# Four groups of row copies ahead of one store, and one load for eight counts

## The chip, the core and the metric

The kernel runs on one core of a Trainium2 chip. The metric is the device time of one execution in microseconds. The core has five engines with instruction streams of their own: TensorE (PE; its weight loads are shown as PEld), VectorE (DVE), ScalarE (ACT), GpSimd (POOL) and SyncE (SP). They wait for each other through semaphores. SP computes nothing: it issues DMA transfers, loads registers and waits. GpSimd issues the gathers whose addresses come from a list of indices.

## The reference

Two graph layers, each added to its input and layer-normed:

```
# layer 0: x (12500,256), 200000 edges src -> dst sorted by dst, 4 heads of 16
ZU = einsum('nd,kdr->knr', Z, U);  zs = ZU[:, src];  zd = ZU[:, dst]
logits = (zs * zd).sum(-1) / sqrt(16)
alpha  = segment_softmax(logits, dst)                  # over the edges of one dst
agg    = segment_sum(alpha[..., None] * zs, dst)
Z_half = 0.5 * Z + 0.5 * einsum('k,knr,kdr->nd', softmax(head_w), agg, U)
DZ = Z_half @ Dmat.T;  residual = Z_half - DZ @ Dmat
x = layernorm(x + relu(Z_half + 0.5 * (residual @ Dmat) - 0.05))
# layer 1: weights from the first 6250 edges' heads, rows xt[dst] of x @ weight
x = layernorm(x + broadcast(einsum('nh,nhd->nd', softmax4(...)[:n], xt[dst[:n]])))
```

What the change touches is the edge part of layer 0: each of the 200000 edges needs the 64 numbers of its source node (256 bytes).

## The kernel before, in words

The edges are cut into tiles of 128 (1563 of them), the nodes into 98 tiles of 128. A *step* pairs one edge tile with one node tile; an edge tile whose edges end in two node tiles has two steps, so there are 1661 steps. The program goes over them in `NB = 52` *blocks* of `B = 32` steps, and a block in `NG = 4` *groups* of `G = 8` steps. Blocks are handled in turn in two halves `h` of every buffer; each engine's code for a block is a function (`period` on TensorE, VectorE and ScalarE, `turn` on SP), and blocks 2 to 47 run in a loop on SP of two blocks a trip (`turn(2 * i + h, ...)`, L483 on), the last four without a loop.

The way of a source row, and who waits for whom:

- GpSimd (L564 to L577) gathers the source rows of an edge tile from the table in DRAM into `ring`, which holds 32 tiles. It gathers in groups `q` of 8. From the fifth on it waits until enough groups of steps have been copied out (`copied`, against a count from the row `frees`).
- SP copies each step's tile from its slot in `ring` to the block's own buffer `zs` (`copy_steps(b, h, g, uses)`, L420 to L444): it waits until TensorE has summed the block before last that far (`sums_ps`), loads the eight slot numbers into registers with one load (L425), loads two counts of gathers (L431, from the row `needs`) and waits for them on the two semaphores `tiles_in` (L434), and issues eight copies (L437). Then it waits for the copies of the group before and raises `copied` for it (`landed`, L415 to L418).
- VectorE (`period`, from L945) makes the head products of the four groups (L902: `zs` times the destination rows in PSUM), then a chain of short steps that goes back and forth with TensorE: running maxima of the logits, at whose end L1012 raises `x_ready`. ScalarE takes the exponentials (L1607), VectorE scans the sums of the block before (L931), weighs `zs` (L1026) and splits it in three bf16 parts (L1031, L1036).
- TensorE expands the destination rows for the head products of the next block (`expand`, L1347, 24 matmuls a group) and adds the weighted rows up by node (`add_up`, L1364), in the order expand 0, expand 1, add_up 0 to 4, expand 2, add_up 4 to 6, expand 3, add_up 6 to 8.
- Beside this runs the dense part of layer 0: each block multiplies two tiles of x (`multiply_x`, L1378); ScalarE copies the product to `xmz` (L1617, raises `xmz_copied`), SP stores it (L471) and loads the next two x tiles (`load_tiles`, L460).

So one turn of SP is, before the change: groups 0 and 1 of block b; wait for `x_ready` of block b-2, load of the block's resets (L453); wait for `xmz_copied` of block b-1, store (L471); load of x tiles (L460); groups 2 and 3. SP works through this in order; a wait holds all that is behind it.

Of the kernel before, what the change touches and what calls it, by code (L numbers as in the profile page):

```python
# [59 lines left out]
G = 8  # L60
NG = B // G
RING = 4 * G
EG = -(-ET // G)
# [34 lines left out]
def spread(ap, axis, n):  # L98

    shape = list(ap.shape)  # L100
    shape[axis] = n
    return ap.broadcast_to(shape)
# [25 lines left out]
def program(nc, x, xT, src_rows, dst_rows, u, dmat, head_w, weight, attn_l, attn_r, out):  # L128
    ctx = ExitStack()
    with ctx:  # L130
# [3 lines left out]
        def sem(name):  # L134
            return ctx.enter_context(nc.semaphore(name))
# [88 lines left out]
        needs = x1T[64:65, :, :].rearrange("a r d -> a (r d)")[:, 0:2 * NB * NG].bitcast(I32)  # L224
# [102 lines left out]
        tiles_in, copied = [sem(f"tiles_in{i}") for i in range(2)], sem("copied")  # L327
# [42 lines left out]
        def rows_of(table, t, n):  # L370

            return table[bass.ds(t * P, n * P), :].rearrange("(t p) c -> p t c", p=P)
# [5 lines left out]
        def last_tiles(engine, lane):  # L378

            last = arow[0:1, (NB - 1) * B:NB * B].rearrange("a (u n) -> a n u", n=NSPARE)[:, lane, 0:LAST // NSPARE]  # L380
            _, tiles = nc.values_load_multi_w_load_instructions(
                last, engines=[engine], min_val=0, max_val=NT + NSPARE,
                skip_runtime_bounds_check_because="the vector engine has clamped the node tile")
            return tiles
# [5 lines left out]
        def _(sp):  # L390
# [24 lines left out]
            def landed(h, g, uses):  # L415

                sp.wait_ge(gathered[h][g], 16 * G * uses)
                sp.nop(nofuse=True).then_inc(copied, 1)  # L418

            def copy_steps(b, h, g, uses):  # L420

                start = type(b) is int and b < 2
                if not start:
                    sp.wait_ge(sums_ps, (B // Q) * (b - 2) + (B // Q // NG) * (g + 1))
                _, slots = nc.values_load_multi_w_load_instructions(  # L425
                    irow[0:1, bass.ds(b * B + g * G, G)], engines=[mybir.EngineType.SP], min_val=0, max_val=RING - 1,
                    skip_runtime_bounds_check_because="the vector engine has made them numbers of slots")
                if start and b == 0 and g == 0:
                    sp.wait_ge(tiles_in[0], 16 * G)
                else:  # L430
                    need = [sp.value_load(needs[0:1, bass.ds((b * NG + g) * 2 + i, 1)], min_val=16 * G, max_val=16 * G * EG) for i in range(2)]  # L431
                    for i in range(2):
                        sp.wait_ge(tiles_in[i], need[i])
                    sp.nop(nofuse=True)  # L434
                here = G if not (type(b) is int and b == NB - 1) else min(G, REAL - b * B - g * G)
                for j in range(here):
                    sp.dma_start(zs[:, h, g * G + j, 0:KR], ring[:, bass.ds(slots[j], 1), :].rearrange("p a c -> p (a c)")  # L437
                                 ).then_inc(gathered[h][g], 16)
                if g >= 1:
                    landed(h, g - 1, uses)  # L440
                elif not (start and b == 0):
                    landed(1 - h, NG - 1, uses - 1 if h == 0 else uses)

            sp.wait_ge(moves_ready, 1)  # L444
            sp.wait_ge(dloc_ready, 1)
            for g in range(2):
                copy_steps(0, 0, g, 1)
            sp.wait_ge(reset_ready, 1)
            sp.dma_start(reset_rows.rearrange("(g p) e -> p g e", p=P), cont[:, :, :]).then_inc(resets_out, 16)
            sp.wait_ge(resets_out, 16)  # L450
# [1 line left out]
            def load_resets(b, h):  # L452
                sp.dma_start(resets[:, h, 0:P], spread(reset_rows[bass.ds(b * B, B), :].rearrange("j (a e) -> j a e", a=1), 1, K)  # L453
                             ).then_inc(resets_in[h], 16)
# [4 lines left out]
            def load_tiles(n, h):  # L459
                sp.dma_start(xe[:, h, :, :], xT[:, :, bass.ds(n * YT * P, YT * P)].rearrange("c p n -> p c n")).then_inc(xe_in[h], 16)  # L460

            def turn(b, h, uses, store, load):

                for g in range(2):
                    copy_steps(b, h, g, uses)
                sp.wait_ge(x_ready, b - 1)
                load_resets(b, h)
                if store:

                    sp.wait_ge(xmz_copied, b - 1)  # L470
                    sp.dma_start(rows_of(xmz_table, (b - 2) * YT, YT), xmz.rearrange("p (t d) -> p t d", t=YT)).then_inc(xmz_out, 16)  # L471
                if load:
                    load_tiles(b - 1, 1 - h)
                for g in range(2, NG):
                    copy_steps(b, h, g, uses)

            for g in range(2, NG):
                copy_steps(0, 0, g, 1)
            sp.wait_ge(prep_read, 6)
            load_tiles(0, 0)  # L480
            for g in range(NG):
                copy_steps(1, 1, g, 1)
            with nc.sync.Fori(1, NB // 2 - 2) as i:  # L483
                for h in range(2):
                    turn(2 * i + h, h, i + 1, True, True)
            for b in range(NB - 4, NB):
                turn(b, b % 2, b // 2 + 1, b - 2 < NY, b - 1 < NY)
# [65 lines left out]
        def _(pool):  # L553
# [29 lines left out]
            for g in range(NG):  # L583
                _, tiles = nc.values_load_multi_w_load_instructions(
                    arow[0:1, b * B + g * G:b * B + (g + 1) * G], engines=[mybir.EngineType.Pool], min_val=0, max_val=NT + NSPARE,
                    skip_runtime_bounds_check_because="the vector engine has clamped the node tile")
                for u in range(g * G, (g + 1) * G):
                    if u >= NSPARE:

                        pool.wait_ge(state_stored, B * b + u - NSPARE + 1)  # L590
                    nc.gpsimd.tensor_copy(acc[:, bass.ds(tiles[u % G], 1), :].rearrange("p a c -> p (a c)"), state_a[:, :, 1 + u]
                                          ).then_inc(state_stored, 1)
# [629 lines left out]
        def _(pe):  # L1222
            T = nc.tensor

            def steps_of(b, g):

                _, tiles = nc.values_load_multi_w_load_instructions(
                    trow[0:1, bass.ds(b * B + g * G, G)], engines=[mybir.EngineType.PE], min_val=0, max_val=NT,
                    skip_runtime_bounds_check_because="the vector engine has clamped the node tile")
                return tiles  # L1230
# [531 lines left out]
```

## Time and profile before

| | before |
|---|---|
| three timed runs, median (lowest to highest) | 3708.65 us (3697.53 to 3719.24) |
| profiled execution: own time, span | 3677.74 us, 3675.2 us |
| busy in the span: PE, DVE, ACT, POOL | 54%, 52%, 32%, 47% |
| mean granted TensorE clock | 0.577 |
| gathers of source rows (L576) | 1563 |
| row copies on SP (L437) | 1660, 32 KB each |

Each line of a timeline gives the start within the span, the duration, the engine (a q behind it: its sequencer, as for a DMA that is issued), the line of the kernel, the operation with what it writes and reads, and in brackets how long the engine had stood and what ended that. Instructions that follow each other at once on one line are one row with a count. In a sum by stretch each engine has its busy time and, in brackets, how many instructions lie in it. The program is the same for every block, so one block can be read for all.

### The profile page before, as it was taken

The numbers are of one execution on the slowest core, as the hardware profiler recorded it, in microseconds if no ns is written. First come the engines' busy times: TensorE is split into PE (matmuls) and PEld (weight loads), VectorE is DVE, ScalarE is ACT, GpSimd is POOL, SyncE is SP. The second block draws the span as 40 slices with busy tenths as digits, with TensorE's granted clock in tenths as the row PEclk, the third lists the DMA queues.
The fourth block names the chain that finished last, engine by engine and source line by source line (L and its number), as shares of the span: only waits on it lengthen the run. The fifth ranks groups of instructions, "written<-read, shape, count | busy, mean of one in ns | idle before, by whom it ended". The sixth has DMA issues, their size and how long they took to land. (4 is left out here: it accounts for less than half of the span.)

```text
span 3675.2 us, 61713 instructions
## 1 busy us (share of the span) xinstructions
PE 1971.2 (54%) x15251; PEld 1490.8 (41%) x15252; DVE 1919.5 (52%) x5864; ACT 1168.6 (32%) x3040; POOL 1728.5 (47%) x1832
## 2 busy tenths in 40 slices
PE   9345545454545445454545455464545454567776
PEld 9233333343434334343424243343433333444666
DVE  4444646454545546454545455464545454666477
ACT  1112323222232323322232233233232322334477
POOL 1544454445444444554544544445544444252662
PEclk7555555555555555555555555555555555577798
DMA  6212222121212212121212112121212121285343
GB/s 205 52 32 46 47 44 46 42 46 42 48 41 47 46 41 48 42 49 40 47 39 48 42 44 48 41 50 41 48 40 45 41 49 39 58 274 179 112 140 107
DMA packets 406593, 232.96 MB, mean 63 GB/s; under 512 B 284096, under 2 KB 371434, under 8 KB 406506
## 3 DMA queue, kind: packets, MB, share of 16 engines
q1 hardware_dynamic: 346666, 154.11, 15.4%
q0 software_dynamic: 59840, 77.87, 9.8%
q8 instruction: 33, 0.54, 0.1%
q14 instruction: 54, 0.44, 0.0%
HBM read 134.80 MB, written 42.55 MB: 48 GB/s over the span
## 5 line engine op out<-in xcount | busy, mean ns | idle before, releaser
L576 POOL DMA_INDIRECT arena<-z_table,sslot x1563 | 1492.0, 955 | 1646.2 <-SPq L418 1114.0
L1347 PE MATMUL bank<-arena 128*128 x4992 | 613.8, 222 | 637.7 <-issue 585.8
L1347 PEld LDWEIGHTS bank<-arena 128*128 128x128 bf16 x4992 | 457.5, 105 | 789.5 <-issue 697.0
L1584 ACT ACTIVATE arena<-bank 128x272 f32<-128x272 f32 x416 | 269.8, 661 | 1574.8 <-remote 970.4
L902 DVE TENSOR_TENSOR xin<-arena,bank 128x512 f32<-128x512 f32 x208 | 143.1, 688 | 1044.3 <-remote 588.2
L1561 ACT ACTIVATE acc<-xTb 128x68 f32 x1600 | 384.6, 312 | 306.6 <-issue 296.0
L1364 PE MATMUL bank<-xto,arena 128*128 128x68 bf16 x3328 | 321.6, 246 | 147.5 <-issue 147.4
L1335 PE MATMUL bank<-ident_b,arena 128*128 128x128 bf16 x1664 | 214.8, 310 | 339.4 <-remote 205.3
L1364 PE MATMUL bank<-arena 128*128 128x68 bf16 x1664 | 296.9, 243 | 120.2 <-issue 90.5
L1364 PEld LDWEIGHTS bank<-xto,arena 128*128 128x128 bf16 x3328 | 281.5, 132 | 166.9 <-issue 166.9
L1335 PEld LDWEIGHTS bank<-ident_b,arena 128*128 128x128 bf16 x1664 | 160.4, 141 | 399.6 <-remote 200.2
L893 DVE TENSOR_SCALAR arena<-iota_b,didx 128x128 bf16<-128x128 bf16 x1664 | 297.9, 263 | 20.2 <-issue 13.4
L931 DVE TENSOR_TENSOR_SCAN xTb<-bank,arena 128x198 f32<-128x198 f32 x612 | 273.2, 522 | 16.2 <-ACT acc L1561 10.3
L1364 PEld LDWEIGHTS bank<-arena 128*128 128x128 bf16 x1664 | 214.1, 129 | 156.8 <-issue 117.9
L1571 ACT ACTIVATE arena<-bank 128x1024 bf16<-128x1024 bf16 x208 | 209.4, 1007 | 83.5 <-remote 52.0
L1378 PE MATMUL bank<-mz,dspace 128*128 128x256 f32 x392 | 183.4, 617 | 0.0
L1031 DVE TENSOR_TENSOR xto<-arena 128x544 f32<-128x544 f32 x208 | 149.3, 718 | 0.0
L905 DVE TENSOR_REDUCE agn<-xin 128x32 f32<-128x512 f32 x208 | 142.7, 686 | 7.2
L1036 DVE TENSOR_TENSOR xto<-xto 128x544 bf16<-128x544 f32 x208 | 145.3, 719 | 0.0
L1026 DVE TENSOR_TENSOR arena<-arena,bank 128x512 f32<-128x512 f32 x208 | 137.5, 681 | 1.8
L632 POOL DMA_INDIRECT xin<-xmz_table,src x98 | 95.4, 973 | 84.8 <-SPq L529 28.2
L1378 PEld LDWEIGHTS bank<-mz,dspace 128*128 128x128 f32 x392 | 109.4, 307 | 16.4
(264 smaller groups left out, 2543.6 us busy)
## 6 DMA issues: line engine op xcount, KB each, us to landing
arena<-arena SPq DMA_DIRECT2D x1660, 32.0 KB
arena<-z_table,sslot POOLq DMA_INDIRECT x1563
dspace<-in_xT SPq DMA_DIRECT2D x49, 256.0 KB
xmz_table<-agn SPq DMA_DIRECT2D x49, 256.0 KB
xmz_table<-arena SPq DMA_DIRECT2D x14, 896.0 KB
arena<-in_x SPq DMA_DIRECT2D x13, 896.0 KB, 11.4
out<-arena SPq DMA_DIRECT2D x12, 896.0 KB
xin<-in_xT SPq DMA_DIRECT2D x8, 896.0 KB
```

What stands on the lines that cost most here:

```text
L576: pool.indirect_dma_start(ring[:, e % RING, :], None, z_table, bass.IndirectOffsetOnAxis(ap=sslot[:, e:e + 1], axis=0)).then_inc(tiles_in[ ...
L893: last = V.tensor_scalar(onehot[:, h, j, :], iota_b[:, :], didx[:, h, j:j + 1], None, ALU.is_equal)
L931: part_done = V.tensor_tensor_scan(to[:, c0:c1, :].rearrange("p c j -> p (c j)"), same_row[:, 0:(c1 - c0) * (B + 1)], sums[:, c0:c1, :].re ...
L1031: V.tensor_tensor(rest[:, js, :], zs[:, h, js, :], top(zs[:, h, js, :]), ALU.subtract).then_inc(rest_ready, 1)
L1036: V.tensor_tensor(low[:, js, :], rest[:, js, :], top(rest[:, js, :]), ALU.subtract).then_inc(parts_ready, 1)
L1335: last = T.transpose(tr_ps[g % 2][:, u * P:(u + 1) * P], onehot[:, h, g * G + u, :], ident_b[:, :])
L1347: last = T.matmul(zd_ps[g % 2][:, u * KR:(u + 1) * KR], onehotT[:, g * G + u, :], z3[:, bass.ds(tiles[u], 1), s, :].rearrange("p a c -> p ...
L1364: last = T.matmul(sum_ps[q % 2][:, (u % Q) * AW:(u % Q + 1) * AW], onehot[:, h, u, :], parts[s][:, u % Q, :], start=(s == 0), stop=(s == Z ...
L1378: last = T.matmul(zd_ps[1][:, t * D:(t + 1) * D], xe[:, 1 - h, c, t * P:(t + 1) * P], mz[:, c, :], start=(c == 0), stop=(c == DC - 1))
L1561: A.activation(acc[:, bass.ds(tiles[u % G], 1), :].rearrange("p a c -> p (a c)"), state[:, :, 1 + u], ACT.Copy).then_inc(state_stored, 1)
L1571: A.activation(onehotT[:, g * G:(g + 1) * G, :].rearrange("p j e -> p (j e)"), tr_ps[g % 2][:, :], ACT.Copy).then_inc(oneT_ready, 1)
L1584: A.activation(sums[:, :, 1 + q * Q:1 + (q + 1) * Q].rearrange("p c j -> p j c"), sum_ps[q % 2][:, 0:Q * AW].rearrange("p (j c) -> p j c", ...
```

## The change

Two edits, both on SP. In `turn`, the store of `xmz` and the load of the x tiles come after groups 2 and 3, where they were before these. And the counts of gathers are no longer loaded in each group, two single loads of one register: a new function `load_needs(b)` loads the eight counts of a block with one load at the start of its turn, and `copy_steps` takes them as an argument.

```
+            def load_needs(b):
+                _, need = nc.values_load_multi_w_load_instructions(
+                    needs[0:1, bass.ds(b * NG * 2, 2 * NG)], engines=[mybir.EngineType.SP], min_val=16 * G, max_val=16 * G * EG)
+                return need
...
-                    need = [sp.value_load(needs[0:1, bass.ds((b * NG + g) * 2 + i, 1)], min_val=16 * G, max_val=16 * G * EG) for i in range(2)]
                     for i in range(2):
-                        sp.wait_ge(tiles_in[i], need[i])
+                        sp.wait_ge(tiles_in[i], need[2 * g + i])
...
             def turn(b, h, uses, store, load):
 
+                need = load_needs(b)
                 for g in range(2):
-                    copy_steps(b, h, g, uses)
+                    copy_steps(b, h, g, uses, need)
                 sp.wait_ge(x_ready, b - 1)
                 load_resets(b, h)
+                for g in range(2, NG):
+                    copy_steps(b, h, g, uses, need)
                 if store:
 
                     sp.wait_ge(xmz_copied, b - 1)
                     sp.dma_start(rows_of(xmz_table, (b - 2) * YT, YT), xmz.rearrange("p (t d) -> p t d", t=YT)).then_inc(xmz_out, 16)
                 if load:
                     load_tiles(b - 1, 1 - h)
-                for g in range(2, NG):
-                    copy_steps(b, h, g, uses)
```

The ends of the program follow: `load_needs(0)` and `load_needs(1)` stand ahead of the first groups of blocks 0 and 1.

SP's program in the loop, before, from the end of group 1 to the first copy of group 2 (names in brackets are the semaphores waited for; ISA is a register instruction; `tspace` holds the slot numbers, `x1T` the counts, `arena` both `ring` and `zs`):

```order
L466 REGISTER_ALU [waits gathered00]
L453 ISA [waits x_ready]
L453 DMA xTb<-reset_rows 128x1x128
L471 ISA [waits xmz_copied]
L471 DMA xmz_table<-agn 128x2x256
L460 ISA
L460 DMA dspace<-in_xT 128x2x256
L424 REGISTER_ALU
L425 ISA [waits sums_ps]
L425 TENSOR_LOAD tspace
L431 ISA
L431 TENSOR_LOAD x1T
```

The same place now:

```order
L473 REGISTER_ALU [waits gathered00]
L459 ISA [waits x_ready]
L459 DMA xTb<-reset_rows 128x1x128
L430 REGISTER_ALU
L431 ISA [waits sums_ps]
L431 TENSOR_LOAD tspace
L442 ISA [waits tiles_in0,tiles_in1]
L442 DMA arena<-arena 128x64
```

The store and the x tiles' load are gone from between groups 1 and 2, and no load of a count stands ahead of the copies. They stand behind group 3, ahead of the next block's group 0:

```order
L442 ISA
L442 DMA arena<-arena 128x64
L480 ISA [waits gathered02,xmz_copied]
L480 DMA xmz_table<-agn 128x2x256
L466 ISA
L466 DMA dspace<-in_xT 128x2x256
L422 ISA
L422 TENSOR_LOAD x1T
L422 ISA x16
L430 ISA
L431 ISA [waits sums_ps]
L431 TENSOR_LOAD tspace
```

What moved there: the wait for `xmz_copied` now comes after all 32 copies of a block, and the 18 instructions at L422 are the one load of eight counts, where each of the four groups had 8 instructions at L431. The programs of the other four engines hold the same instructions in the same order.

## Rows read from the trace of the kernel before

**Rows 1.** Waits of SyncE, 300 to 3210: total us, times, longest us.
```profile
SPq L471 <- ACT agn L1617: 282.2, 34, 18.9
...
SPq L425 <- PE bank L1364: 1.6, 5, 0.5
```

**Rows 2.** Waits of all engines over the same stretch.
```profile
POOL arena L576 <- SPq L418: 1046.2, 131, 21.1
```

**Rows 3.** Line 902, head products: min/median/max ns, first and last start.
```profile
L902 DVE TENSOR_TENSOR xin<-arena,bank x208: 686/687/690, 162.5 to 3204.8; 128x512 f32<-128x512 f32 x104
```

**Rows 4.** Timeline, VectorE, one block: start us, us, instruction, count, idle before.
```profile
2236.45 0.69 DVE L902 TENSOR_TENSOR xin<-arena,bank 128x512 f32<-128x512 f32 x1 [0.21 <-DVE fac L1054]
...
2262.90 0.69 DVE L902 TENSOR_TENSOR xin<-arena,bank 128x512 f32<-128x512 f32 x1 [19.87 <-PE bank L1347]
...
2281.61 0.29 DVE L1012 TENSOR_TENSOR xin<-bank,xin 128x128 f32<-128x128 f32 x1
...
2296.62 0.69 DVE L902 TENSOR_TENSOR xin<-arena,bank 128x512 f32<-128x512 f32 x1 [0.65 <-DVE fac L1054]
```

**Rows 5.** Timeline, the DMA queue's engine in that block.
```profile
2233.53 5.16 SPq L437 DMA_DIRECT2D arena<-arena  x8
...
2241.50 7.61 SPq L437 DMA_DIRECT2D arena<-arena  x8
...
2262.70 5.09 SPq L437 DMA_DIRECT2D arena<-arena  x8
...
2270.71 10.58 SPq L437 DMA_DIRECT2D arena<-arena  x8
```

**Rows 6.** Timeline, ScalarE and TensorE in that block.
```profile
2235.97 1.35 ACT L1584 ACTIVATE arena<-bank 128x272 f32<-128x272 f32 x2 [10.64 <-PE bank L1364]
...
2242.91 1.45 PE L1347 MATMUL bank<-arena 128*128 x11
```

**Rows 7.** Sums by stretch: busy us (x starts), clock, DMA share, GB/s.
```profile
core 0: us, PE busy (x) PEld busy (x) DVE busy (x) ACT busy (x) POOL busy (x), PEclk, DMA share, GB/s
2234.20:2244.50 10.30, 9.88 (x114) 8.45 (x114) 6.17 (x11) 2.66 (x4) 3.78 (x4) 0.50 0.23 48
2244.50:2262.40 17.90, 1.93 (x9) 0.94 (x9) 0.00 (x0) 0.65 (x1) 11.35 (x12) 0.50 0.16 31
2274.70:2280.70 6.00, 0.00 (x0) 0.00 (x0) 0.23 (x3) 0.96 (x3) 2.88 (x4) 0.50 0.17 38
2287.20:2294.00 6.80, 3.39 (x22) 2.22 (x23) 6.70 (x14) 0.00 (x0) 4.14 (x4) 0.63 0.39 101
```

**Rows 8.** Timeline, GpSimd: the first gather of each run.
```profile
2239.53 0.95 POOL L576 DMA_INDIRECT arena<-z_table,sslot  x1 [7.63 <-SPq L418]
...
2268.69 0.96 POOL L576 DMA_INDIRECT arena<-z_table,sslot  x1 [9.46 <-SPq L418]
...
2282.20 0.94 POOL L576 DMA_INDIRECT arena<-z_table,sslot  x1 [3.71 <-SPq L418]
```

**Rows 9.** The page's costliest groups: the gathers of source rows.
```profile
L576 POOL DMA_INDIRECT arena<-z_table,sslot x1563 | 1492.0, 955 | 1646.2 <-SPq L418 1114.0
```

**Rows 10.** Line 431, a load of one count on SyncE.
```profile
L431 SPq TENSOR_LOAD <-x1T x414: 2/272/1385, 117.9 to 3186.9; - x138
```

**Rows 11.** Another block: timeline of VectorE and GpSimd, and a sum by stretch.
```profile
1822.86 0.69 DVE L902 TENSOR_TENSOR xin<-arena,bank 128x512 f32<-128x512 f32 x1 [0.65 <-DVE fac L1054]
...
1862.72 0.29 DVE L1012 TENSOR_TENSOR xin<-bank,xin 128x128 f32<-128x128 f32 x1
...
1880.76 0.29 DVE L1020 COPY arena<-bank 128x128 f32<-128x128 f32 x1 [6.20 <-remote]
...
1888.99 0.69 DVE L902 TENSOR_TENSOR xin<-arena,bank 128x512 f32<-128x512 f32 x1 [0.21 <-DVE fac L1054]
...
1862.87 0.95 POOL L576 DMA_INDIRECT arena<-z_table,sslot  x1 [0.30 <-SPq L418]
...
1862.50:1879.50 17.00, 5.75 (x39) 4.19 (x38) 6.33 (x17) 1.43 (x3) 11.41 (x13) 0.70 0.17 33
```

More of the change, by code:

```diff
@@ L418, in landed, with copy_steps @@
                 sp.nop(nofuse=True).then_inc(copied, 1)
-            def copy_steps(b, h, g, uses):
+            def load_needs(b):
+                _, need = nc.values_load_multi_w_load_instructions(
+                    needs[0:1, bass.ds(b * NG * 2, 2 * NG)], engines=[mybir.EngineType.SP], min_val=16 * G, max_val=16 * G * EG)
+                return need
+            def copy_steps(b, h, g, uses, need):
                 start = type(b) is int and b < 2
@@ L445, in _ @@
             sp.wait_ge(dloc_ready, 1)
+            need = load_needs(0)
             for g in range(2):
-                copy_steps(0, 0, g, 1)
+                copy_steps(0, 0, g, 1, need)
             sp.wait_ge(reset_ready, 1)
@@ L473, in turn @@
                     load_tiles(b - 1, 1 - h)
-                for g in range(2, NG):
-                    copy_steps(b, h, g, uses)
             for g in range(2, NG):
-                copy_steps(0, 0, g, 1)
+                copy_steps(0, 0, g, 1, need)
             sp.wait_ge(prep_read, 6)
             load_tiles(0, 0)
+            need = load_needs(1)
             for g in range(NG):
-                copy_steps(1, 1, g, 1)
+                copy_steps(1, 1, g, 1, need)
             with nc.sync.Fori(1, NB // 2 - 2) as i:
```

## The prediction

> **What bounds the kernel now.** I read four views, and then one block instruction by instruction. First the waits of the DMA queue's own engine, SyncE (SP). Over the whole loop it waits for one thing only, the x product's copy on ScalarE: 282.2 us in 34 waits; the counts that the row copies wait for cost it next to nothing [rows 1]. So SP is never early with its row copies. The waits of all engines say the same from the other side: GpSimd (POOL) stands 1046.2 us, 131 times, waiting for SP's signal that ring slots are free [rows 2]. Up to here this looks like a kernel that SP bounds, and the change takes work off SP.
>
> The second half of the reading says otherwise. Take one ordinary block. The first head product of the block starts at 2236.45, the first of the next at 2296.62: 60.2 us, near the mean (3042.3 us from the first to the last head product [rows 3], over 51.75 blocks, is 58.8). I call 2236.45 time 0. VectorE has made three of the four head products by +6.6 and then stands 19.87 us, until +26.5, for the fourth; the subtraction that the exponentials wait for (L1012, which raises x_ready) comes at +45.2 [rows 4]. SP had issued the eight copies for that fourth product by +12.7 (2241.50 and 7.61 us [rows 5]), and TensorE had all but the last matmuls of its expansion running from +6.5 [rows 6]. What stands between is in the sums by stretch: from 2234.2 to 2244.5 TensorE starts 114 matmuls in 10.3 us; from 2244.5 to 2262.4 it starts 9 in 17.9 us, VectorE starts nothing, ScalarE one instruction, and only POOL goes on, with 12 gathers. The same from 2274.7 to 2280.7: no matmul, three VectorE instructions, POOL four gathers [rows 7]. POOL's gathers explain the edges: a run of gathers begins at 2239.53 and the engines stall 5.0 us later; sixteen gathers at 1.25 us (955 ns each [rows 9] and 0.30 us idle between two [rows 11]) end at 2259.2, and they recover at 2262.4; the next run begins at 2268.69, and TensorE is out from before 2274.7 to 2280.7 [rows 7, 8]. A copy on SP costs 0.65 us outside such a stall (eight in 5.16 and 5.09 us) and about 1.3 us in one (eight in 10.58 us) [rows 5]. So I read the period as fast time plus stalls, and a stall as the tail of a run of gathers: the first 5 us of a run are free, the rest and some 2 to 3 us behind it are not. A run of 8 (9.7 us) stalls some 7 us, a run of 16 (19.7 us) some 17. The clock plays no part: 0.50 granted, the 1.2 GHz level, in stall and fast stretch alike [rows 7].
>
> The third run of this block, at 2282.20, costs little: from 2287.2 to 2294 VectorE is busy 6.70 of 6.8 us [rows 7], since it falls on the long weighing instructions. Where a run falls, and whether two become one, decides the period, and SP's signals place the runs, since POOL starts 0.84 us after SP ends a group of eight copies (2238.69 to 2239.53 [rows 5, 8]).
>
> **The change part by part.** *Loads of the counts.* Per block go 4 groups of 8 register instructions (2 of them loads); 18 instructions (one load) come, ahead of group 0. Between the groups at 2233.53 and 2241.50 SP spends 2.81 us [rows 5]; the removed eight are 2 loads of median 0.272 us [rows 10] and six short ones, I take 1.4 us together in fast time (bounds: 0.54 for the loads alone; 2.81 for all that lies there). The new 18 stand behind the x tiles' load, where SP then waits for sums: cover about 4 us; bare they cost 18 times some 0.1 to 0.7 us, 2 to 12 us, the low end in fast time. I cost them at nothing. Of the saved 5.6 us nothing shortens the block by itself, as SP is not what VectorE stands for.
> The Trainium skill, "DMA: Bandwidth & Descriptors", section "Latency and other measured facts", gives a register load a floor of about 600 ns. Seven loads fewer would be 4.2 us a block by it; the row has 0.272 us, and the measurement decides.
>
> *Groups 2 and 3 ahead of the store.* Before, SP's order after a store is groups 2, 3 of a block, then 0, 1 of the next. Now it is 0, 1, 2, 3 of one block, and group 0 waits for the block before last to have been summed. ScalarE takes the first eighth of the sums at 2235.97, -0.5 [rows 6], the second 0.7 us later, so group 0 is released at +0.2 where group 2 before started at -2.9. Plus 1.4 us of registers and 5.2 of copies: it ends at +6.8, POOL's first run starts at +7.6. With the third run gone from the end of the block the sums may be 2 us earlier; I take +6.6 (before +3.1).
> The stall then begins at +11.6. The fourth expansion, 11 matmuls in 1.45 us from 2242.91 [rows 6], would be through all 24 at +9.7, so the fourth head product is made before the stall, not behind it. Its copies are there from the block before: this is the gain of the move, 2.0 us of chain (two instructions of 0.7 and the next scan).
> *First run.* Group 1 follows group 0 by at most 10.4 us even with the old loads (2.81 and 7.61), which is inside POOL's 10.0 plus its 0.84; so the first run stays one of 16, ends at +26.3, and the engines recover at about +29.3 (before +26.0).
> *Second run.* Before, a group ends 5.4 us after recovery (2262.70 and 5.09). Now it has the 8 fewer, five for the resets: about +4, at +33.3; POOL starts at +34.1. The last group took 2.92 and 10.58, 13.5 us, so that POOL had finished its 8 and stood 3.71 us [rows 8]. Take 1.4 from the registers, and the two copies that so move into fast time save 0.7 each: 10.7 us, hence POOL finds its signal as it ends the eighth gather. The gap of 3.71 us closes: a run of 16, to +53.8, recovery at +56.3. Of the chain 12.7 us are then made in the window from +29.3 to about +40 (10.7 and the 2.0 from above); in this block it takes 12.8 from fourth head product to L1012 without the stall (18.7 less 5.9). So x_ready just comes through.
> *What such a block takes* the trace has already: there the second run is 1 and 15 gathers (1862.87 joins, 0.30 idle), L1012 is made at 1862.72, VectorE is released at 1880.76, the next block begins 8.2 us on, at 1888.99, and the block lasts 66.1 us; TensorE made 39 matmuls in the 17 us [rows 11]. With 8.2 after +56.3 I get 64.5 us, 4.3 more than 60.2.
>
> **The sum.** 1563 gathers are 195.4 groups over 52 blocks, 3.76 a block: 39 blocks have four groups, 13 have three. 39 times 4.3 is +168 us. A block of three has no pair to join and keeps the 2 to 3 us of the earlier head product: 13 times -3 is -39. Together +129 us on the profiled execution's 3677.74, that is 3807; that execution is 31 us under the median 3708.65, so in its terms **3838 us**.
>
> **The rivals.** *The last group stays late* (faster). If it still ends 12 us or more behind POOL's start, the runs stay 16, 8, 8, the third lies under the weighing as now, and only the earlier fourth product counts: -2.5 us in each of 52 blocks, 3579 us; decided by whether POOL idles 2 us or more between its second and third run. [...] Against: the same group with fewer registers starts where copies are quick.
> *SP bounds after all* (much faster). SP never waits but for the x product; that wait (282.2 over 49 blocks, 5.8) goes, and some 3.6 us of registers (5.6 less 2): -9.4 us a block, 3250 us. Against: VectorE's long wait outlasts its copies by 13 us. The Trainium skill, "Perfetto Trace Analysis", section "Optimizing DMA Performance", calls a kernel bound by its DMA sequencer where the issuing engine's track is solid DMA slices; SP's row of 32 copies is such a track, and by that rule this rival is right. The stretches without matmuls speak against it.
> *x_ready just misses* the window (slower, a worse form of mine): L1012 comes at +57 and the next block 15 us later, 72 us; 39 times 11.6, less 39, gives 4120.
> *Nothing moves*: the runs only change places in the block, 3709.
>
> **Chances.** Mine 0.40 and its worse form 0.15, last group late 0.22, SP bound 0.08, nothing 0.15. Its own range is 3740 to 3950. The 8 in 10 range takes in the late group and part of the worse form: 3560 to 4020. A measurement of this kernel tells about 0.5% from no change. Faster by over 0.5%: 0.31; within: 0.14; slower: 0.55.
>
> **What would show it.** In the changed profile: SP's wait for the x product stays or grows, but nothing is queued behind it; the fourth head product starts about +10; POOL's waits for SP fall from about 2.5 to 2 a block, with runs of 16; the stretch without matmuls in the middle of a block is twice 17 us. Wrong if POOL idles 2 us or more between its second and third group, if the fourth head product still stands 20 us, or if engines start instructions at their usual pace in the middle of a run of gathers.

## The result and the profile after

The changed kernel takes 4056.65 us, the median of three runs (4056.23 to 4060.92), against 3708.65 (3697.53 to 3719.24): a ratio of 1.094, 95% interval 1.089 to 1.100. The forecast was 3838 in a range of 3560 to 4020; the direction was right, the size 219 us short. The profiled execution's span is 4054.7 us, that of before 3675.2: 379.5 us more.

They are in the block. From the first to the last head product it is 3435.4 us instead of 3042.2 [rows 3]. Over the 48 blocks 2 to 49 I took the distance from one first head product to the next and counted as one *run* all gathers that follow each other with under 0.6 us between; a run belongs to the block in which it begins, from 3 us ahead of the first head product on. Before, the mean block is 59.5 us, and 24 of the 48 have runs of 16, 8 and 8 (60.0 us on the mean); after, it is 67.8 us, and 24 have two runs of 16 (71.2 us).

The waits of SP after, over the same part of the program (columns as in [rows 1]: total us, times, longest):

```profile
SPq L480 <- ACT agn L1625: 886.3, 47, 23.6
SPq L431 <- PE bank L1372: 134.1, 50, 13.0
SPq L431 <- remote: 41.6, 12, 14.1
SPq L439 <- DMA arena<-z_table,sslot: 32.3, 31, 2.3
```

SP now stands 886.3 us for the x product, where it stood 282.2 [rows 1]: SP has more slack than before, not less. GpSimd waits for SP's signals less often and longer, and VectorE has one long wait that was small before (L1005, L997 before, 80.4 us in 11 waits there). `remote` is what the profile writes where it finds no releaser:

```profile
POOL arena L584 <- SPq L418: 1440.5, 96, 28.0
DVE xin L910 <- remote: 927.8, 43, 34.3
DVE back L1005 <- remote: 367.7, 32, 16.6
```

96 waits instead of 131 [rows 2] are 1.9 a block instead of 2.5: runs have joined. Two neighbouring blocks of the changed kernel show what this costs, since the first has its second run joined and the next has not. GpSimd, the first gather of each run:

```profile
2314.07 0.94 POOL L584 DMA_INDIRECT arena<-z_table,sslot  x1 [21.56 <-SPq L418]
2340.40 0.94 POOL L584 DMA_INDIRECT arena<-z_table,sslot  x1 [6.67 <-SPq L418]
2385.43 0.94 POOL L584 DMA_INDIRECT arena<-z_table,sslot  x1 [25.14 <-SPq L418]
2411.79 0.94 POOL L584 DMA_INDIRECT arena<-z_table,sslot  x1 [6.69 <-SPq L418]
```

VectorE (L910 the head products, L1005 a scan late in the chain, L1020 the subtraction that raises `x_ready`):

```profile
2310.16 0.69 DVE L910 TENSOR_TENSOR xin<-arena,bank 128x512 f32<-128x512 f32 x1 [0.65 <-DVE fac L1062]
...
2337.95 0.69 DVE L910 TENSOR_TENSOR xin<-arena,bank 128x512 f32<-128x512 f32 x1 [22.35 <-remote]
...
2347.17 0.16 DVE L997 COPY ccol<-bank 128x1 f32<-128x1 f32 x1 [1.92 <-remote]
...
2363.55 0.56 DVE L1005 TENSOR_TENSOR_SCAN back<-rnext,bank 1x32 f32<-1x32 f32 x4 [13.96 <-remote]
...
2366.49 0.29 DVE L1020 TENSOR_TENSOR xin<-bank,xin 128x128 f32<-128x128 f32 x1
...
2381.05 0.69 DVE L910 TENSOR_TENSOR xin<-arena,bank 128x512 f32<-128x512 f32 x1 [0.21 <-DVE fac L1062]
...
2409.26 0.69 DVE L910 TENSOR_TENSOR xin<-arena,bank 128x512 f32<-128x512 f32 x1 [22.76 <-remote]
...
2423.84 0.56 DVE L1005 TENSOR_TENSOR_SCAN back<-rnext,bank 1x32 f32<-1x32 f32 x4 [2.78 <-remote]
...
2426.78 0.29 DVE L1020 TENSOR_TENSOR xin<-bank,xin 128x128 f32<-128x128 f32 x1
...
2441.77 0.69 DVE L910 TENSOR_TENSOR xin<-arena,bank 128x512 f32<-128x512 f32 x1 [0.65 <-DVE fac L1062]
```

The two are alike up to the fourth head product (+27.8 and +28.2). Both second runs begin 2.5 us behind it. In the first block it is 16 gathers, and VectorE, 2.94 us of chain short of `x_ready`, stands 13.96 us; in the second it is 8, and VectorE stands 2.78 us. The blocks take 70.9 and 60.7 us: 10.2 us for the eight gathers that joined. SP's row copies of both blocks (each row is two groups):

```profile
2308.14 11.88 SPq L442 DMA_DIRECT2D arena<-arena  x16
...
2328.25 20.39 SPq L442 DMA_DIRECT2D arena<-arena  x16
...
2379.40 11.97 SPq L442 DMA_DIRECT2D arena<-arena  x16
...
2401.64 19.85 SPq L442 DMA_DIRECT2D arena<-arena  x16
```

and the sums by stretch (columns as in [rows 7]) of the first stall, of the second, and of the same place in the block with the short run:

```profile
2322.50:2335.50 13.00, 1.08 (x5) 0.51 (x5) 0.00 (x0) 0.65 (x1) 8.49 (x9) 0.50 0.18 35
2346.00:2363.50 17.50, 1.96 (x14) 0.93 (x11) 2.35 (x11) 2.31 (x8) 10.94 (x12) 0.50 0.14 27
2412.00:2424.00 12.00, 4.66 (x29) 2.79 (x28) 7.35 (x37) 4.84 (x18) 7.42 (x8) 0.50 0.22 44
```

14 matmuls in 17.5 us in the second stall. The granted clock is 0.50, the 1.2 GHz level, in all three, so the clock makes none of the difference.

### The profile page after: what moved, and what is told of

The parts are those of the page before. It is cut to its first block, busy times and chain, and to the rows that moved or that the text cites. A ratio compares the mean times of both kernels' runs of the same rounds, so it can differ in the third digit from the quotient of the medians.

```text
span 4054.7 us, 61056 instructions
## 1 busy us (share of the span) xinstructions
PE 1965.1 (48%) x15251; PEld 1487.9 (37%) x15252; DVE 1917.3 (47%) x5864; ACT 1179.5 (29%) x3040; POOL 1717.9 (42%) x1832
## 4 chain that ended last, share of the span: by engine, by line
another core or an unknown queue 40%; DVE 33%; PE 14%; issue 9%; ACT 3%; ACTq 1%; DVEq 0%; DMA 0%; POOL 0%; POOLq 0%; SPq 0%
DVE xTb L939 7%; DVE arena L901 6%; PE bank L1355 5%; DVE xto L1039 3%; DVE xto L1044 3%; DVE xin L910 2%; DVE arena L1034 2%; PE bank L1510 2%; DVE agn L913 2%; PE bank L1480 1%; DVE carry L991 1%; PE bank L1500 1%; ACT arena L1669 1%; PE bank L1512 1%
## 5 line engine op out<-in xcount | busy, mean ns | idle before, releaser
L910 DVE TENSOR_TENSOR xin<-arena,bank 128x512 f32<-128x512 f32 x208 | 143.0, 687 | 1071.9 <-remote 938.1
L1355 PE MATMUL bank<-arena 128*128 x4992 | 572.1, 224 | 155.8 <-DVE xin L910 78.2
L1372 PE MATMUL bank<-xto,arena 128*128 128x68 bf16 x3328 | 348.6, 244 | 448.7 <-issue 448.7
L1005 DVE TENSOR_TENSOR_SCAN back<-rnext,bank 1x32 f32<-1x32 f32 x208 | 29.0, 195 | 389.5 <-remote 378.9
```

Source lines behind the costliest of these rows:

```text
L910: V.tensor_tensor(prod[:, :, :], zs[:, h, g * G:(g + 1) * G, 0:KR], zd_ps[g % 2][:, :].rearrange("p (j c) -> p j c", j=G), ALU.mult).then_ ...
L1355: last = T.matmul(zd_ps[g % 2][:, u * KR:(u + 1) * KR], onehotT[:, g * G + u, :], z3[:, bass.ds(tiles[u], 1), s, :].rearrange("p a c -> p ...
L1372: last = T.matmul(sum_ps[q % 2][:, (u % Q) * AW:(u % Q + 1) * AW], onehot[:, h, u, :], parts[s][:, u % Q, :], start=(s == 0), stop=(s == Z ...
```

## The experiments

All ratios are to the kernel before, run on the same chip in the same rounds. The first six kernels part the change, the other nine ask what a stall hangs on. An expectation names theories by letters; A is always that runs of gathers stall the other engines.

**Each edit alone.** `e1_order_only`:

```
                 load_resets(b, h)
+                for g in range(2, NG):
+                    copy_steps(b, h, g, uses)
                 if store: ...
                 if load: ...
-                for g in range(2, NG):
-                    copy_steps(b, h, g, uses)
```

> The kernel before with one edit of the two: groups 2 and 3 stand ahead of the store, the counts are still loaded group by group. Theory A (a run of gathers on GpSimd stalls the other engines from some 5 us after its start to some 2.5 us behind its end, and two runs of 8 joined into one of 16 cost the period about 10 us): in the kernel after, SyncE ends its last group at +38.5 and raises the signal at +39.3, where GpSimd ends its eighth gather of the second run at +40.3, so the runs join with 1 us to spare. The count loads put 1.4 to 2.8 us between those two, so about half of the blocks or more should stay apart: 3750 to 3950 us, waits of GpSimd for SyncE between 96 and 131. Theory B (the place of the store decides alone: every block as after): 4020 to 4080, and about 96 waits. Theory C (SyncE's own time bounds the loop): the added loads make it slower than the kernel after, over 4080.

3788.94 us, ratio 1.031 (1.024 to 1.038): in theory A's range, with 119 waits, but not for its reason. Only 2 of the 48 blocks are (16, 16); 23 are (16, 8, 8), and these take 64.0 us instead of 60.0. One of them, on VectorE:

```profile
1319.27 0.69 DVE L902 TENSOR_TENSOR xin<-arena,bank 128x512 f32<-128x512 f32 x1 [0.21 <-DVE fac L1054]
...
1328.52 0.69 DVE L902 TENSOR_TENSOR xin<-arena,bank 128x512 f32<-128x512 f32 x1 [3.01 <-PE bank L1347]
1350.60 0.42 DVE L970 TENSOR_TENSOR_SCAN xin<-xTb,bank 128x128 f32<-128x128 f32 x1 [20.49 <-remote]
...
1368.44 0.29 DVE L1012 TENSOR_TENSOR xin<-bank,xin 128x128 f32<-128x128 f32 x1
```

Its first run begins at 1327.35, +8.1 (median of all blocks +8.3; +3.4 before). The fourth head product is at +9.2, before the stall, as the prediction had it; but the 20 us wait is only passed on to the next scan (L970, with L905 and a TensorE step between), and since the run begins 5.0 us later than in [rows 8] (+3.1), it ends at +31.3 instead of +26.5. Making an instruction before a stall is worth nothing when the same move puts the stall's end later.

`e2_loads_only`: `load_needs` and the eight counts by one load, groups 2 and 3 behind the store as before.

> The other edit alone: one load of eight counts, the store and the x tiles' load stand between groups 1 and 2 as before. Theory A: the gap of 3.7 us between the second and the third run shrinks by 1.4 to 2.8 us but stays open in most blocks, so the period hardly moves: 3650 to 3780 us, 115 to 135 waits of GpSimd for SyncE. If it joins instead, some 39 blocks cost 10 us more: about 4050 and 96 waits. Theory C (SyncE's own time bounds): 1.4 to 2.8 us off each of four groups, 50 blocks: 3150 to 3430.

3898.12 us, ratio 1.060 (1.053 to 1.067): outside all ranges, nearest the joined case. 28 of 48 blocks are (16, 16) with 67.8 us, and there are 96 waits. I had put the gap at 3.7 us and the saving at 1.4 to 2.8; nothing of the gap was left. So the loads edit joins the runs by itself. 1.031 times 1.060 is 1.093, near the 1.094 of both, and the place of the first run adds up too: its median start is +3.4 before, +8.3 with the order alone, -1.1 with the loads alone and +4.3 with both. The order edit moves it 5 us later in either case. The price of that in joined blocks is 3.4 us (67.8 with the loads alone, 71.2 with both).

**The runs parted again.** `e3_signal_held` is the kernel after with:

```
+                if g == NG - 1 and not start:
+                    sp.wait_ge(x_ready, b)
+                    sp.nop(nofuse=True)
                 if g >= 1:
                     landed(h, g - 1, uses)
```

> The kernel after, with one wait more: in group 3 SyncE waits, after its eight copies, until the block that is being computed has raised x_ready, and only then raises the signal of group 2. So GpSimd's second run is 8 gathers, and the third starts behind x_ready, under the weighing. Nothing is taken from SyncE's work; it waits more. Theory A: the joined runs were the whole loss, so the time comes back to that of the kernel before or a little better: 3600 to 3760 us; x_ready at about +45 instead of +56, block about 60 us. Theory B (SyncE or the store's late place bounds): a wait more in SyncE's program makes it slower than the kernel after, 4057 to 4400.

3721.73 us, ratio 1.012 (1.004 to 1.021). This is in theory A's range. A wait more on SP takes back nearly all of the loss: 25 blocks are (16, 8, 8) with 61.7 us, and the median of x_ready is +46.2 instead of +55.4. SP as the bound is ruled out.

`e8_loads_held` is the same wait on top of loads-only.

> The one load of eight counts alone (store between groups 1 and 2 as before), and the signal of group 2 held until x_ready as in the kernel after with the held signal. Loads only made 28 of 48 blocks two runs of 16 with 67.8 us. Theory A: with the runs apart the block is that of before (60.0) less the 1 to 3 us that the shorter loads take from group 2's start and from the second run's: 3560 to 3700 us, at or below the kernel before. Theory C (the single load itself, 18 instructions at the head of the turn, costs what loads-only lost): no return, 3850 to 3950.

3922.82 us, ratio 1.062 (1.056 to 1.068): nothing. That was my mistake, not the load's price: in this order group 3 is copied in the next block, after x_ready of its period has risen, and 25 blocks stayed (16, 16). The signal that joins the runs there is group 0's. `e9_signal0_held` holds that one:

```
+                if g == 1 and not start:
+                    sp.wait_ge(x_ready, b)
+                    sp.nop(nofuse=True)
```

> The one load of eight counts alone, with the signal of group 0 (which SyncE raises in group 1, and which starts the second run) held until x_ready. The trace of loads-only shows the second run released at +27.5 to +29.2 by group 0 and joined by group 1's signal, so that this is the pair to part; a wait in group 3 found x_ready already raised and changed nothing. Theory A: x_ready no longer stands behind the second run (+35 to +45 instead of +52), the second run starts behind x_ready, and since group 1 is long copied, it is one run of 16 under the weighing and into the next block: 3450 to 3750 us. Theory F (the single load's 18 instructions at the head of the turn cost what loads-only lost): 3850 to 3950.

3624.01 us, ratio 0.988 (0.979 to 0.997). The time is in theory A's range, the form is not: the second run still begins at about +31, released by the signal before, but as 8 gathers, and the third behind x_ready (27 blocks of (16, 8, 8), 59.5 us). So the one load shows no cost of its own: with the runs apart the kernel is, if anything, 1% faster. Order with loads (1.012) against loads alone (0.988), both held: the intervals don't meet, some 2.4% between them. The first run begins at +7.0 in the one and at +2.0 in the other (medians), so this fits the late first run of `e1_order_only`; the two hold different signals, though, so it is not the order edit alone that parts them.

**The other direction.** `e7_pairs` joins the runs in the kernel before, on GpSimd, with SP untouched:

```
-                    pool.wait_ge(copied, ... frees[0:1, q - 4:q - 3] ...)
+                    if q % 2 == 0:
+                        f = min(q + 1, EG - 1) - 4
+                        pool.wait_ge(copied, ... frees[0:1, f:f + 1] ...)
```

> The kernel before, where GpSimd waits for ring slots only once for two groups of gathers, for the later of the two: every run is 16 gathers, and SyncE's program is that of before, store and loads of counts included. Theory A (two runs of 8 joined cost some 10 us a block, whatever joined them): 3950 to 4150 us, about 98 waits for SyncE. Theory E (it is where a run falls, not its length): the joined run of the second half starts 12 us later than now, behind x_ready, and lies under the weighing; the block stays 60 us or falls: 3500 to 3750. Theory B (the store's place made the loss): no change, 3690 within 1%.

3927.61 us, ratio 1.061 (1.054 to 1.068), a little under A's range and far from E's and B's. 31 blocks are (16, 16) with 69.6 us. Here x_ready is not late (+43.8, median of the 31); the second run starts at +40.2, and the loss comes behind x_ready: 23.0 us from there to the next block, 14.9 in the (16, 8, 8) of before. So a run of 16 is not hidden under the weighing as one of 8 was. Part of the loss may be another: this kernel also gathers later, and VectorE's head products waited 375.7 us for row copies (300 to 3210), 17.3 before. The run does not part the two.

**What of a gather stalls the others.** `e5_few_rows` fetches 16 rows instead of 128 (`ring[0:16, ...]`, `sslot[0:16, ...]`) from the fifth group of gathers on, in the kernel after; the other 112 rows of a tile stay as they were, so it serves for the time alone.

> The kernel after, with gathers that fetch 16 rows instead of 128 from the fifth group of gathers on (the other 112 rows of a tile are left as they were, so the output is not the reference's); the count of gathers, signals and waits is the same. Theory A: what stalls the engines is GpSimd's work on a gather. If its time goes by rows, a run of 16 lasts 16 times some 0.4 us and the stall nearly vanishes: the block falls to 30 to 45 us, 2400 to 3100 us in all, and SyncE's copies become what bounds. If the time of a gather is mostly fixed (near 0.95 us still), the stall stays and so does the time: over 3900. Theory C (SyncE or the copies' queue bounds, the gathers only happen to lie there): no change, 3950 to 4080, although the gathers are short.

4072.61 us, ratio 1.104 (1.096 to 1.112), the time of the kernel after. The page's line of the gathers and one stall:

```profile
L585 POOL DMA_INDIRECT arena<-z_table,sslot x1563 | 1322.1, 846 | 2199.0 <-SPq L418 1553.6
```

```profile
1468.00:1482.00 14.00, 1.29 (x6) 0.52 (x5) 0.00 (x0) 0.04 (x1) 9.11 (x11) 0.50 0.06 14
```

The transfers are at 14 GB/s and a DMA share of 0.06 (35 and 0.18 in the stall of the kernel after), and TensorE still starts only 6 matmuls in 14 us. So it is not the fetched data. A gather of an eighth of the rows takes 846 ns instead of 949; as its time stayed, this run does not part theory A from C, which `e3_signal_held` did.

**Breaking the runs.** In four kernels GpSimd waits within a run until the gathers so far have landed: `e6_twos` and `e6_fours` in the kernel after, `e10_twos_before` in the kernel before:

```
                 for e in range(q * G, min((q + 1) * G, ET)):
+                    if e > q * G and e % 2 == 0:     # 4 in the fours
+                        pool.wait_ge(tiles_in[q % 2], 16 * (G * (q // 2) + e - q * G))
```

and `e11_fours_all` also ahead of each eight (`pool.wait_ge(tiles_in[(q - 1) % 2], 16 * G * ((q - 1) // 2 + 1))`).

> The kernel after; ahead of the fifth gather of each eight GpSimd waits until the four before have landed. No run is longer than 4 gathers (some 5 us), and between two lies one landing, some 2 us. Theory A (the first 4 to 5 us of a run cost the others nothing, what follows does): the engines are hardly stalled any more; the block falls to 40 to 55 us, bound by GpSimd itself (8 gathers and two landings, some 14 us, times 3.76) or by SyncE's copies: 2700 to 3500 us. Theory D (a gap must be as long as the recovery, 2.5 us or more, and one landing is too short, so four and four count as one run): the joined runs stay and are 4 us longer, 4100 to 4250. Theory C (SyncE bounds, gathers don't matter): 4057 and the like.

> The kernel after; GpSimd waits for the landing after every second gather. 30 gathers a block in pairs of 2.5 us and a landing of some 2 us: 4.5 us a pair, 68 us a block for GpSimd alone. Theory A: no stalls, the gathers' own pace bounds: 60 to 70 us a block, 3700 to 4100, and the head products, x_ready and all that is between come without long stands of VectorE (no idle time over 6 us put down to a matmul). Theory D (gaps of a landing are too short): runs of 16 of 36 us that stall for all their length, over 5000.

> The kernel before, where GpSimd waits for a landing after every second gather, as in the run of pairs with the kernel after (3425 us, ratio 0.925 to before). Theory A: with the runs broken up, GpSimd's own pace (14.3 us a group of 8) bounds, and the change between before and after is worth almost nothing: 3380 to 3480 us, within 1.5% of the 3425. Theory B (the store's place or the loads carry a cost of their own): the loss of 9% stands between the two here too, 3130 us for this one, or if the gain came from the loads, 3550 and more.

> The kernel after, with a landing awaited ahead of every fourth gather, also at the start of each eight, where the run of fours had left 4 and 4 joined. All runs are 4 gathers (5 us) with 1.7 us idle between. Theory A (the first 4 to 5 us are free, one landing's gap is enough to begin anew): GpSimd's pace is 12.8 us a group, 51 us a block of four; 3050 to 3350 us. Theory D (a gap must outlast the recovery of 2 to 3 us, and what counts is the share of time that GpSimd works on gathers): fours stall as before, 3500 to 3650, no better than the run of fours (3594).

| kernel | us | ratio (95%) | VectorE's head products waited longest for |
|---|---|---|---|
| e6_fours | 3594.46 | 0.973 (0.966 to 0.980) | remote |
| e6_twos | 3424.91 | 0.925 (0.919 to 0.931) | the row copies |
| e10_twos_before | 3411.11 | 0.930 (0.922 to 0.938) | the row copies |
| e11_fours_all | 3337.44 | 0.906 (0.897 to 0.915) | the row copies |

`e6_fours` missed A's range: the last four gathers of one eight and the first four of the next still joined into runs of 8, and those stall; theory D's range was missed as well. (The two kernels of twos have the same join: their runs are 2, 2, 2 and then 4 with the next eight's first.) With that join gone (`e11_fours_all`) the time is 7% lower, at the top of A's range. `e6_twos` missed A's range on the fast side. `e10_twos_before` is the sharpest: before and after, 9% apart, are the same (0.930 and 0.925, overlapping intervals) once the runs are broken. So nothing of the 9% is left then. GpSimd's pace bounds these two, though, so a small price on SP would not show in them.

The last four fill the gap with work of GpSimd in place of a landing, on the kernel after (`e12_short_gaps` four memsets behind every second gather, `e13_one_memset` one behind every second, `e14_fours_memsets` four behind every fourth, `e15_each` one behind every gather):

```
+                    if e % 2 == 1:
+                        for _ in range(4):
+                            nc.gpsimd.memset(pacer[:, :], 0.0).then_inc(paced, 1)
+                            n_paced += 1
+                            pool.wait_ge(paced, n_paced)
```

> The kernel after, with four small memsets of GpSimd (128x8, each awaited) behind every second gather in place of the wait for its landing: pairs of gathers with a shorter gap, some 0.8 to 1.2 us more idle time of the gathers' unit instead of 1.45. Theory A (a gap in the gathers is enough, whatever fills it): a group of 8 takes 13 to 15 us, and the time is that of the pairs or some per cent below, 3250 to 3480. Theory G (it is the landing that frees the others, that is the transfers in flight; or GpSimd's being idle): other work of GpSimd in the gap does not help, 3700 to 4100.

> The kernel after with one memset of GpSimd (some 0.15 us) behind every second gather instead of four (0.60 us, which gave 3239 us and 13.3 us a group of 8). Theory A1 (the length of the unbroken run counts, any work of another kind breaks it): no stalls, a group takes 11.5 us and the block 46 to 50: 2950 to 3180 us. Theory A2 (the gap must be long enough to refill, about 0.5 us or more): the stalls come back in part or whole, 3350 to 4050.

> The kernel after with four memsets (0.60 us) behind every fourth gather. Runs of 4, 5 us long, a group of 8 in 12.2 us. Theory A1: 5 us are free, so no stalls, and the shorter group gives 49 to 51 us a block, 3030 to 3200. Theory A2 (each gap gives back a fixed amount, so what counts is gap time per gather): half the gap time of the pairs, stalls in part: 3300 to 3700.

> The kernel after with one memset (some 0.15 us) behind every gather. Runs of one, gap time per gather between that of the two others: a group takes 12 to 13 us. Theory A1: 3050 to 3250. Theory A2 with a least gap of some 0.5 us: the stall stays, 3500 to 4100; with gap time per gather as the measure (0.15 against 0.15 for fours with four memsets): the same as that run within 2%.

| kernel | gathers between gaps | gap | gap ahead of the next eight | us | ratio (95%) |
|---|---|---|---|---|---|
| e12_short_gaps | 2 | 0.88 | 1.94 | 3238.58 | 0.881 (0.874 to 0.889) |
| e14_fours_memsets | 4 | 0.88 | 1.94 | 3525.96 | 0.954 (0.947 to 0.961) |
| e15_each | 1 | 0.39 | 1.47 | 3857.24 | 1.045 (1.039 to 1.051) |
| e13_one_memset | 2 | 0.39 | 1.48 | 3908.71 | 1.059 (1.055 to 1.064) |
| after | 16 (8) | 0.30 between any two | 0.30 if joined | 4056.65 | 1.094 (1.089 to 1.100) |

The gap is the time from the end of one gather to the start of the next (medians). Ahead of each eight, where GpSimd also loads a count and waits for `copied`, it is longer in all four than the memsets alone make it. So no run there is longer than an eight, and `e13_one_memset` and `e15_each` have runs of 8 that are broken by 0.39 us only. The timeline of GpSimd in `e12_short_gaps`:

```profile
1505.92 1.00 POOL L588 DMA_INDIRECT arena<-z_table,sslot  x1 [0.27 <-POOL pacer L592]
1507.22 0.95 POOL L588 DMA_INDIRECT arena<-z_table,sslot  x1 [0.30 <-issue]
1508.17 0.61 POOL L592 MEMSET pacer<- 128x8 f32 x4
1509.05 1.03 POOL L588 DMA_INDIRECT arena<-z_table,sslot  x1 [0.27 <-issue]
```

and in `e15_each`:

```profile
1501.92 0.95 POOL L588 DMA_INDIRECT arena<-z_table,sslot  x1 [0.27 <-POOL pacer L592]
1502.87 0.12 POOL L592 MEMSET pacer<- 128x8 f32 x1
1503.26 1.05 POOL L588 DMA_INDIRECT arena<-z_table,sslot  x1 [0.27 <-issue]
```

A gap of 0.88 us after two gathers (0.61 of memsets and 0.27) removes the long stalls, one of 0.39 us hardly helps, even after each single gather. Work of GpSimd serves as well in the gap as waiting. By the expectations: `e12_short_gaps` came 11 us under theory A's range, `e13_one_memset` and `e14_fours_memsets` in A2's, and `e15_each` in that of a least gap, while gap time per gather as the measure is out (9% between `e15_each` and `e14_fours_memsets`). VectorE's waits in the two with pairs, over their loops, first `e12_short_gaps`, then `e13_one_memset`:

```profile
DVE xin L919 <- DMA arena<-arena: 646.3, 63, 14.0
...
DVE xin L919 <- remote: 71.9, 10, 12.4
```

```profile
DVE xin L919 <- remote: 724.9, 36, 32.2
DVE xin L987 <- remote: 271.2, 29, 17.7
```

In the first VectorE waits for row copies, that is for gathers not yet made. GpSimd waited for SP once, 1.4 us, in the whole loop (300 to 2700): its own pace, 13.5 us for eight, now bounds. `e12_short_gaps` beats both kernels, by 11.9% and, over the shared reference, by 19% (0.881 to 1.094).

## Why the prediction was right and where it was wrong

*The bound.* Right. SP did not bound (rival at 3250): its waits grew, and a wait more took time off. The page that the prediction set against this does not say otherwise. By the Trainium skill, "Perfetto Trace Analysis", section "Optimizing DMA Performance", a sequencer's track of solid DMA slices marks a bound. SP's track is solid only within a group of eight, 28.4 of the block's 60.2 us [rows 5], so by that rule SP is not the bound either, and the runs agree.

*Loads at nothing.* Right as to their own price (`e9_signal0_held`), but I priced their effect on the gap only together with the order. The loads alone close it.

*First run at +6.6.* It begins at +3.9. The formula for the order (copies from +0.2, 1.4 of registers, 5.2 and 0.84: +7.6) is what `e1_order_only` does, +8.1. In the changed kernel the sums of the block before last come earlier, and the formula's 1.0 us for that is too little: ScalarE takes the first at 2306.63,

```profile
2306.63 1.35 ACT L1592 ACTIVATE arena<-bank 128x272 f32<-128x272 f32 x2 [7.42 <-PE bank L1372]
```

which is -3.5 (-0.5 in [rows 6]). Most of this fits the third run that is gone from the block's end: with the loads edit but the third run kept, the first begins at +7.0 (`e3_signal_held`), only 1.3 us ahead of `e1_order_only`.

*Fourth head product ahead of the stall.* Failed, and by the rule itself, "the first 5 us of a run are free". By it the stall of a run from +3.9 begins at +8.9. TensorE had the fourth expansion through at +8.4, ahead of that, and SP had issued the copies for this product in the block before, by 2279.92:

```profile
2315.47 3.13 PE L1355 MATMUL bank<-arena 128*128 x24
```

```profile
2260.96 18.96 SPq L442 DMA_DIRECT2D arena<-arena  x16
```

The kernel has the fourth product wait for these two alone, and yet VectorE starts nothing from 2315.60 to 2337.95. So a run stops the product earlier than it stops TensorE's matmuls; whether VectorE is held or TensorE's signal comes late, the trace does not tell. Over the 48 blocks the fourth expansion ends at +8.4 to +8.9 in all but one. In the four where the run had begun at most 1.4 us before that end, the product follows within 0.1 us; in all 43 where it had begun 2.7 us or more before, the product comes 3.4 to 31 us late. In `e1_order_only` the border is the same: up to 2.1 us (41 blocks) it follows at once, and in the four with 2.9 to 3.5 us it comes 6.7 to 20 us late. So for this product hardly 3 us of a run are free. The 2.0 us of chain were not there, and where the order did put the product ahead, `e1_order_only` gained nothing.

*Second run joined.* Right: SP ends the last copies at +38.5 and signals them 0.8 us later, GpSimd ends its eighth gather at +40.1.

*x_ready just comes through.* This is the step that failed, and the term that it mis-sized is the +4.3 us of a joined block. Of 12.8 us of chain I wanted 2.0 made ahead of the first stall and 10.7 in the window between the stalls. Measured in the block above, the window is 11.6 us (2337.95 to 2349.59), but the chain behind the fourth product takes 14.6 us without the long stall: the 2.0 are not made ahead, and VectorE already stands 1.92 us at L997, 4.8 us into the second run. So 2.94 us are left when it stops, x_ready has to wait for the end of the stall, and the block takes 70.9 us instead of 64.5. The missing fourth product is the smaller part: the four blocks that had it at +8.5 or +8.6 took 69.1 us on the mean against 71.2, and in three of them x_ready still came behind the second run (+54.3 to +55.0). This is the rival "x_ready just misses" (72 us, 4120).

*The sum.* I put 39 blocks of four groups at +4.3 and 13 of three at -3. Of the 48 blocks measured, the 37 with 32 gathers went from 60.8 to 70.5 us, +9.7, and the 11 with 24 from 55.3 to 58.4, +3.1: together 394 us. Both terms were off, the second in its sign.

*Last group late* (3579 us, -2.5 a block): its form, runs of 16, 8 and 8, was made in `e1_order_only` and `e3_signal_held`, and it cost +4.0 and +1.7 us a block. The gain that I saw in its earlier fourth product is not there, even where that product is early (median +10.8 in both): the first run, and with it the end of its stall, comes later by more.

*Open.* Why a run stalls the other engines. They start little while GpSimd makes gathers back to back, it is neither the clock nor the volume of data, and of the gaps tried after every second gather 0.88 us let them go on and 0.39 us did not. Why the head product is held sooner than the matmuls is open too. Whether what they lack then is their instructions was not tried.

## What to carry to other kernels

When every engine but one is silent in a stretch, line the edges up with the one that works before believing any named wait. Work taken off an engine with slack is not free: it moves signals, and here two signals 1 us too close cost 10 us a block. If GpSimd's gathers come in runs, spread them: a gap of 0.9 us after every second one gave 12%, more than any order of SP's program that was tried here. And a rule for when a stall begins, read on one engine, need not hold for another.

## What the runs showed of the hardware

- A gather of 128 rows of 256 bytes keeps GpSimd 949 ns, one of 16 rows 846 ns: in this pattern the time is nearly fixed, and 0.30 us lie between two.
- Runs of gathers with 0.30 or 0.39 us between hold all other engines; with 0.88 us after every two they go on, after every four only in part (3526 against 3239 us), though the runs are just 5 us long. The landing's gaps of `e11_fours_all`, 1.7 us after every four and 2.8 ahead of each eight, do better (3337). So the "first 5 us free" of the prediction is not a property of each short run: the gap counts as much as the run's length.
- The kernels' order by time is not that of the gathers' share of time alone: `e15_each` leaves GpSimd 0.39 us after each gather and `e14_fours_memsets` 0.88 after each fourth and 0.30 else, about the same sum (4.2 and 4.6 us for eight, with the gap ahead of the next), at 3857 and 3526 us. Here one longer gap was worth more than four short ones.
- A run holds VectorE's head product sooner than TensorE's matmuls: products whose inputs were ready did not start once a run of gathers had gone on for 2.7 us or more (43 blocks of the kernel after), while TensorE still made 24 matmuls in 3.13 us up to 4.5 us into the run.
